# A software pipeline over batches: four streams in one loop turn

## The reference

```
x = x + gdn(layernorm(x));  x = x + ffn(layernorm(x))

gdn(x):  q, k, v = silu(conv4(x @ Wq)), silu(conv4(x @ Wk)), silu(conv4(x @ Wv))   # 16 heads x 64
         q, k = unit(rope(q)), unit(rope(k))
         beta = sigmoid(x @ bw + bb); alpha = exp(-exp(A_log) * softplus(x @ gkw + gkb + dt_bias))
         for each token t:                                                # S: 64 x 64 per head
             o[t] = q[t] @ S + D * sum(q[t] * k[t]) * v[t]
             S = alpha * (S - beta * outer(k[t], k[t] @ S)) + beta * outer(k[t], v[t])
         return ((x @ Wg) * silu(rmsnorm(o) * onorm_w)) @ Wo

ffn(x):  h = ln1(x);  x = x + softmax(q k^T / sqrt(8)) v @ Wo             # 16 heads x 8
         m = ln2(x);  p = softmax(m @ Wg);  top 2 of 8 experts, weights normed
         return x + sum_e w_e * (gelu(m @ W1[e] + b1[e]) @ W2[e] + b2[e])
```

## Time and profile before

| | us |
|---|---|
| median of three runs (7421.98 to 7423.77) | 7421.99 |
| profiled execution | 7428.07 |
| its span | 7426.3 |
| from one turn's copy into xnT to the next (from 442.83, 672.88, 901.52) | 228.7 in the mean |

### The profile page before, as it was taken

One profiled execution on the slowest core, in us unless ns is written; L12 is line 12 of the kernel. 1 busy time (PEld: TensorE's weight loads), 2 busy tenths in 40 slices (PEclk: granted clock), 3 DMA queues, 4 the chain that ended last, 5 costly groups with the idle time before them and its releaser, 6 DMA issues.

```text
span 7426.3 us, 126059 instructions
## 1 busy us (share of the span) xinstructions
PE 5379.1 (72%) x40448; PEld 3830.1 (52%) x40448; DVE 4707.4 (63%) x11688; ACT 3031.4 (41%) x5605; POOL 2662.2 (36%) x2990
## 2 busy tenths in 40 slices
PE   4677776777767777777777677776777767777767
PEld 2455554555544555445555455554455544555545
DVE  5765567655676655676556765567665567655672
ACT  3444434444344433444443444434444344443343
POOL 3443234433334332344333443333433234433341
PEclk6687776777767777677777677776777767777767
DMA  2000000000000000000000000000000000000000
GB/s 66 2 2 3 3 2 2 3 3 3 3 1 3 3 3 3 2 2 3 3 3 2 2 3 3 3 2 2 3 3 3 3 1 3 3 3 3 2 2 3
DMA packets 26460, 29.73 MB, mean 4 GB/s; under 512 B 4072, under 2 KB 22768, under 8 KB 25328
## 3 DMA queue, kind: packets, MB, share of 16 engines
q1 hardware_dynamic: 25712, 20.49, 0.9%
HBM read 16.29 MB, written 4.19 MB: 3 GB/s over the span
## 4 chain that ended last, share of the span: by engine, by line
PE 34%; issue 33%; POOL 16%; DVE 14%; ACT 2%; POOLq 1%; DVEq 0%; SPq 0%; ACTq 0%; DMA 0%
PE bank L855 33%; POOL NP L589 4%; POOL Gam L617 4%; POOL Gam L614 4%; DVE Gam L1381 3%; POOL NP L586 2%; DVE NP L1257 2%; DVE NP L1390 2%; DVE hn L1243 1%; POOL NP L592 1%; POOL frstd L655 1%; PE bank L859 1%; ACT Gam L744 1%; ACT NP L690 1%; DVE Gam L1409 1%
## 5 line engine op out<-in xcount | busy, mean ns | idle before, releaser
L855 PE MATMUL bank<-QK 64*128 64x256 f32 (+1 forms) x4096 | 883.7, 420 | 206.2 <-ACT pT L818 100.2
L1257 DVE SCALAR_TENSOR_TENSOR NP<-bank,conv_w,NP 128x255 f32<-128x255 f32 (+2 forms) x2304 | 929.5, 470 | 77.4 <-ACT NP L690 77.4
L842 ACT ACTIVATE QK<-bank,b 128x256 f32<-128x256 f32 x1024 | 419.7, 470 | 923.7 <-PE bank L855 923.1
L855 PEld LDWEIGHTS bank<-QK 64*128 64x128 f32 (+1 forms) x4096 | 324.9, 158 | 717.6 <-ACT pT L818 254.6
L855 PE MATMUL bank<-xnT,Wqkv 128*128 128x256 f32 x1536 | 609.4, 546 | 101.3 <-DVE NP L1257 53.4
L1575 DVE SCALAR_TENSOR_TENSOR moe<-bank,wsel,moe 128x128 f32<-128x128 f32 x512 | 156.0, 346 | 771.6 <-PE bank L855 771.6
L855 PE MATMUL bank<-mT,W 128*128 128x256 f32 x2048 | 574.8, 434 | 0.0
L855 PE MATMUL bank<-NP,head_cols 128*32 128x256 f32 x1536 | 204.1, 478 | 488.2 <-POOL NP L586 488.1
L690 ACT ACTIVATE NP<-bank,conv_b,conv_w 128x256 f32<-128x256 f32 x768 | 388.7, 556 | 357.1 <-PE bank L855 356.9
L855 PEld LDWEIGHTS bank<-xnT,Wqkv 128*128 128x128 f32 x1536 | 384.1, 271 | 284.1 <-DVE NP L1257 117.5
L855 PE MATMUL bank<-W,QK 128*128 128x128 f32 x4096 | 505.2, 276 | 22.5 <-DVE moe L1575 22.5
(11 more groups left out here) (212 smaller groups left out, 11098.9 us busy)
## 6 DMA issues: line engine op xcount, KB each, us to landing
xin<-in_x SPq DMA_DIRECT2D x33, 128.0 KB, 2.1
out<-moe SPq DMA_DIRECT2D x32, 128.0 KB, 2.5
W<-in_W SPq DMA_DIRECT2D x1, 2048.0 KB
NP<-in_c_q_sel SPq DMA_DIRECT2D x1, 1536.0 KB, 8.2
NP<-in_c_k_sel SPq DMA_DIRECT2D x1, 1536.0 KB, 11.4
NP<-in_c_alpha_sel SPq DMA_DIRECT2D x1, 1024.0 KB, 4.9
Wqkv<-in_Wq SPq DMA_DIRECT2D x1, 512.0 KB, 12.2
Wqkv<-in_Wk SPq DMA_DIRECT2D x1, 512.0 KB, 12.8
```

Source lines behind the costliest of these rows:

```text
L842: ins = s.activation(h1[:, n % 2, f, :], ps[:, q, :], ACT.Gelu_apprx_tanh, bias=b1[:, n, f:f + 1])
L855: return mm(out_, lhsT, rhs, start=first, stop=last)
L1257: v.scalar_tensor_tensor(acc[:, n % 2, m, j:T], ps[:, m, 0:T - j], conv_w[:, kind, c, PAD - j:KT - j], acc[:, n % 2, m, j:T], ALU.mult, AL ...
```

## The change

One loop turn now holds four streams, each of another batch: `LAG` puts the front (norm, gate, the eight qk steps) one batch ahead, the v steps and the back (heads, block steps, tail) at batch i, attention (and the gated output) at i − 1, experts at i − 2. The back stream is the spine. The table `SIDE` names, for each of its milestones, the steps of the other streams that every engine issues there. The turns run from −1 to 33: −1 has the front alone, 2 to 30 hold all streams (3 to 29 in the loop), 31 to 33 end the last batches.

- The back has three banks: alpha in bank 0, kk in 1 and 2 in turn, later uses in rotation over 0 to 2. All qk and v steps use bank 3; gate, alphaT, sums, vT bank 4; attention and experts 5 to 7 as before. A bank has one signal "full" for each stream.
- `W1` and `W2` hold two experts. SP loads an expert's 256 KB + 256 KB again in each turn once its buffer is free (the up and the down of the expert two before are done).
- `xnG`, a copy of `xnT` (128 KB), and `QK1`, a copy of the second half of `QK` (1 MB), are made by SP's DMA each turn. They serve v, g and the products with the state, while the front writes the next `xnT` and `QK`. SP also loads `x1` from memory in place of GpSimd's copy.
- `acc`, `rot`, `sq`, `sumsT`, `h1` have their own SBUF; yT lies over `pT`. The cos product is written straight to `QK`. `layer_norm` is split into statistics and application. The rep products use 32 rows.
- The blocks are brought into Z by one 128-row transpose and two copies on ScalarE, instead of four 32-row transposes (L1424).

```diff
+LAG = {"front": -1, "V": 0, "back": 0, "attn": 1, "experts": 2}
+BACK_BANKS, CONV_BANK, MISC_BANK = 3, 3, 4
+def back_uses():
+    uses = [(("alpha", 0), "v_Gam", 1, 0)]
+    for c in range(NC):
+        uses += [(("kk", h), "v_NP", h + 1, 1 + h % 2) for h in (2 * c, 2 * c + 1)]
+        uses += [(("alpha", h), "v_Gam", h + 1, 0) for h in (2 * c + 1, 2 * c + 2) if h < H]
...
+SIDE = (
+    ("start", steps("front", ("stat", 0))),
+    (("head", 1), steps("attn", ("norm", 0)) + steps("experts", ("up", 0))),
...
+    (("head", 10), steps("V", ("v", 0)) + steps("experts", ("up", 2), ("down", 1)) + steps("attn", ("Wo", 0))),
...
+    (("block", 21), steps("experts", ("down", 6)) + steps("front", ("silu", 0)) + steps("attn", ("mrow", 3))
+      + steps("front", ("qk", 2), ("silu", 1)) + steps("attn", ("att", 0)) + steps("front", ("rope", 0))
+      + steps("experts", ("down", 7)) + steps("attn", ("att", 1))),
...
+    (("o", 1), steps("front", ("rope", 6))),
+    ("end", steps("attn", ("mT", 0)) + steps("front", ("rope", 7)) + steps("attn", ("router", 0), ("wT", 0),
+      ("b2", 0)) + steps("front", ("sums", 0))),
+)
...
-        W1 = sb("W1", [P, NE, FF])
+        W1 = sb("W1", [P, 2, FF])
-        W2 = sb("W2", [P, NE, NF, HID])
+        W2 = sb("W2", [P, 2, NF, HID])
+        xnG = sb("xnG", [P, T])
+        QK1 = sb("QK1", [P, NC, 2, P])
...
-        def batches(eng, gdn, ffn, first=lambda: None):
-            first()
-            gdn(0, alone)
-            eng.wait_ge(loaded_ffn, 16 * len(loads_ffn))
-            if B > 1:
-                gdn(1, beside(ffn, 0))
-            if B > 2:
-                with eng.Fori(2, B) as i:
-                    gdn(i, beside(ffn, (i, 1)))
-            beside(ffn, B - 1)(None)
+        def turns(eng, back, side):
+            def one(i):
+                now[0], indices, taken = i, turn(i), [0]
+                def meanwhile(milestone):
+                    if milestone is not None and milestone not in MILESTONES:
+                        return
+                    end = len(SIDE) if milestone is None else MILESTONES.index(milestone) + 1
+                    for _, items in SIDE[taken[0]:end]:
+                        for stream, step, n in items:
+                            if indices[stream] is not None:
+                                side[stream](indices[stream], step, n)
+                    taken[0] = max(taken[0], end)
...
+                if m is not None:
+                    for e in range(2, NE + 2):
...
+                        hold(*full_at(m, ("h1", e - 2, 1)))
+                        hold(*full_at(m, ("y", e - 2)))
+                        expert(e % NE)
+                    hold(v_moe.sem, v_moe.at(m, v_moe.per))
+                    sp.dma_start(out_rows(i[0] - 2 if isinstance(i, tuple) else m), moe[:]).then_inc(out_stored.sem, 16)
```

More of the change, by code:

```diff
@@ L544, in _ @@
+            for i in range(-1, min(3, B + 2)):
+                one(i)
+            if B > 5:
+                with sp.Fori(3, B - 2) as i:
+                    one((i, 0))
+            for i in range(max(3, B - 2), B + 2):
+                one(i)
             sp.wait_ge(out_stored.sem, out_stored.at(B, 0))
@@ L665, in _, with experts @@
+            def experts(m, step, n):
+                pass
+            turns(pool, back, {"front": front, "V": values, "attn": attn, "experts": experts})
         @block.scalar
@@ L813, in ffn @@
                         .then_inc(a_QK6.sem, 1)
[L814 removed]
+                elif step == "att":
                     act.wait_ge(*full_at(j, ("st", n)))
@@ L844, in ffn @@
                         ins.then_inc(a_h1.sem, 1)
-            batches(act, gdn, ffn)
+            turns(act, back, {"front": front, "V": values, "attn": attn, "experts": experts})
         @block.tensor
@@ L1377, in gdn, with back @@
+            def back(i, meanwhile):
+                norms(i)
+                dve.wait_ge(*full_at(i, "GT"))
+                v.tensor_copy(Gc[:].rearrange("p a h -> p (a h)"), bank("GT")[:, 0:2 * H]).then_inc(v_Gc.sem, 1)
+                meanwhile("start")
+                before = turn(now[0])["attn"]
                 for h in range(H + 1):
@@ L1577, in ffn @@
                     ins.then_inc(v_moe.sem, 1)
-            batches(dve, gdn, ffn, lambda: normalise_x(0))
+            turns(dve, back, {"front": front, "V": values, "attn": attn, "experts": experts})
 def tables():
```

980 lines of the change are left out of this document (550 added, 430 removed).

## The result

The changed kernel took 7069.69 us in the median of three runs (7063.89 to 7073.93), against 7421.99 before: a ratio of 0.9524, with an interval of 0.9502 to 0.9545. It is 352 us faster, where 218 us slower was forecast. The profiled execution's span is 7067.6 us.

A forecast was written before the change was run, and what follows sets the result against it. No single engine bounds the kernel: each of five stretches has its own bound, 74 to 93% full. 67 + 82 + 75 + 10 = 234 us a turn; 862 + 29 × 234 = 7648, + 1.8 − 6: 7640 us; range 7000 to 8000.

The forecast's parts named there:

- Heads: Start and heads of a full turn: eight pairs 34 us, side work 25, start 2.5, K transposes 4; 67 with rounding.
- the pair's period: Heads: with two kk banks a head pair takes 4.2 us at the high clock, 5.3 at the low, instead of 2.74.
- the 25 us of side work on the path: Heads: of 33 us of experts, Wo, v product, y transposes and gate, 25 lengthen the turn; least 11, most 33.
- Block steps: Block steps with convs and maxima on VectorE 58 us, attention behind 20.5, qk convs 3.5: 82, where 42 stood.
- Tail: Turn 0's 66.7 us at clock 0.52, −3.5 for fewer Z transposes, +12 for side work on TensorE: 75 us.
- End: End of a turn: the router's serial chain, mostly small VectorE operations, now stands uncovered: 10 us, at the least 4.
- Ends: Partly filled turns at start and end of the program: 862 us together, where they cost 569 before.
- The rule and the rivals: Tail: the skill's rule that gapless TensorE keeps its high clock was set aside for turn 0's row of 0.52.
- Rival 1: Clock stays high through blocks and tail: tail 52 for 75, 207 us a turn, 6845 us; chance 0.14.
- Rival 2: Side work hides better than summed: 208 to 220 us a turn, about 7150 us; chance 0.19.
- Rival 3: Heads run at the low clock: 42 us for pairs, ups 3.3 each, 251 us a turn, 8140 us; chance 0.18.
- Transfers: Streamed expert weights and copies on SP's queue: nothing to 6 us a turn, 1 taken.

The follow-up runs named there:

- the hint: The changed kernel with a back-edge hint for the loop's branch on every engine: 7055.12 us.
- two near variants of the same tail: The kernel before with 96 unused products ahead of turn 0's tail (7421.17 us), and with two banks for kk instead of four (7827.71 us).

## Why the prediction was wrong

- **What bounds the kernel, and the sum of stretches.** The method held: the stretches of the changed kernel are the ones forecast, and they do follow each other.
- **Heads: right.** 67 forecast, 67.1 measured, and the pair's period confirmed by itself (4.32 and 5.38). The total is in part luck: the granted clock was 0.74 in the first 28 us, below the 0.89 that I took, and xn's 3.7 us of waiting for GpSimd weren't in the sum. So the other terms together, most of all the 25 us of side work on the path, must have been too large by about as much; they weren't measured one by one.
- **Block steps: 6 us too long.** The sum up to the last row of maxima is right (58 forecast; from 3542.9 to 3599.5, 56.6). The 24 us for attention behind it are 19 until VectorE's last block step, since attention's last heads run beyond the end of the block steps.
- **Tail: 21 us too long, and this is the step that failed.** I took the tail's length and its clock from turn 0, as the only tail that lay bare. The arithmetic on it (−3.5, +12) was for the low clock. TensorE was busy 49.8 us in the changed tail where my sum had about 70; 20 of the 21 us are that. The row was real and not typical: of the 32 tails in that trace it is the only one whose g products took 5.28 us and not 3.60. The rows of a full turn said so too: the clock of 1.00 from 2687 on the earlier trace rows I put down to the experts, and the tail without side steps has the same rise without any. With 54 for 75 the sum would have been 213 a turn and 7035 us, within 0.5% of what was measured; that it comes so near is luck in part, since the block steps' error and the end's cancel.
- **End: 8 us too short.** 10 forecast from the last batch's end, where GpSimd had nothing else to do and no loop ends. In the loop the two things that aren't in those rows add 3.4 (hn beside GpSimd, 4.41 for 0.99) and 2.6 (the branch), and each goes when its cause is taken away. The remaining 2 us or so are the way from g's end to hn and from the branch to the first kk product. The branch was there to be read in the kernel before, on ScalarE: it idled ahead of the copy into xnT, 63.3 us at 29 places, and TensorE waited 3.00 us for that copy (2731.46) against 0.81 where no branch stands ahead (443.33).

```profile
2730.96 0.37 ACT L717 COPY xnT<-bank 128x256 f32<-128x256 f32 x1 [2.10 <-issue]
```

- **Ends: 862 forecast, 833 measured.** They hold the same tail term in three turns, 62 us too much, and nothing for the 22.6 us in which TensorE waits for weights in the last turns. The rest of the difference isn't broken down.
- **The rule and the rivals.** Rival 1 had the right mechanism, with 0.14 of the chances: it gave 207 us a turn and 6845 us, for a clock high throughout. The clock is at 0.72 in the first part, so about 20 of its 23 us came true in the tail. Rival 2 (side work hides better) names the right time, 7150 with 208 to 220 a turn, by terms that aren't what happened: heads 56.5, block steps 72, tail 72 and end 7, where 67, 76, 54 and 18 were measured. Only its block steps are near, and the tail is short by the clock and not by hidden side work. The Trainium skill's rule ("TensorE: Matmul & The Clock Gate", "Why this matters for your kernels") that a TensorE without gaps gets its high clock was the better guide here than my row. It isn't the whole either: turn 0 before is without a gap of over 0.9 us from 179 to 217, and its clock is at 0.50 until 215. Rival 3 (heads at the low clock) is partly true and costs less than it said: three of the six ups in the heads are slow (3.55, 2.95 and 3.21 us for 1.9), and yet the heads took the 67 us of the forecast.
- **Transfers, breakeven.** 1 us a turn taken, nothing measured in full turns, 27 us at the end of the program. The turn had to come under 226 us; it came to 215. The convs' 65 us are off the path and the tail and end together are 19 shorter (91 to 72), while heads and block steps are 70 longer (73 to 143).

## What to carry to other kernels

Take no stretch's time, and above all no TensorE clock, from a single turn: look how long the same products take in all other turns of the trace (g: 3.60 us in 31 of 32) before one row stands for them. When work is laid beside other work, look at pairs of engines that exclude each other (GpSimd's SBUF multiplications and VectorE's SBUF operations here, 198 us), and at idle time without a waited-for event, such as that at the loop's branch: in the kernel before it stood on another engine. Divide a cost by the number of turns only after looking where it lies (the waits for weights were all at the end). A saving of 2 us in a turn may be given back by the clock, so judge it by the whole time and not by the gap that it closed.

## What of the hardware was unexpected

- A wait of 1.7 us of TensorE in a stretch at full clock was followed by 20 us at the low clock without a gap (the version with the earlier router), in every turn from 1 on: 68 us of time over the kernel, although the end had got 9 us shorter a turn. A wait as long 11 us earlier was followed by no fall.
- The rise of the clock in the tail came at different products: at V,Z in the changed kernel, 11 us later in most turns with the hint, behind S,QK without side steps. In turn 0 of the kernel before it came in one profiled execution only at the end, and in two near variants of the same tail 28 and 32 us after the join's first product.
- VectorE's 128x128 operations took 0.3 us alone and up to 2.5 us beside GpSimd's 128x1024 multiplications, in both forms tried, while operations with an input in PSUM kept their time; a 128x4 operation took 1.70 us for 0.15. Beside GpSimd's power over 128x32 (5.42 us) VectorE's operations kept theirs.
- VectorE idled 2.6 to 3.0 us at each of 26 loop ends (70.2 us in all), and 0.4 with the hint.
